# When VectorE adds a left tile to the running sum: a step after TensorE's use of it, or a step ahead of it

## What is computed

```python
x = x + ref(gn(x))
def ref(x, g_w, g_b, W_w, W_b, gamma, beta):
    g_x = einsum('oc,bchw->bohw', g_w, x) + g_b      # values, 128 channels
    f = einsum('bnc,bcm->bnm', theta, phi)           # theta = phi = x, 4096 x 4096
    attn = softmax(f, axis=-1)
    y = einsum('bnm,bmc->bnc', attn, g_x)
    wy = einsum('oc,bchw->bohw', W_w, y) + W_b
    wy = batchnorm(wy) * gamma + beta
    return wy + x
```

## Time and profile before

| | |
|---|---|
| time, median of 3 runs | 2401.73 us (2400.95 to 2404.8) |
| the profiled execution's own time | 2396.38 us |
| its span, first to last instruction | 2394.6 us |
| TensorE matmul busy | 2170.7 us, 91% |
| VectorE busy | 1690.0 us, 71% |
| ScalarE busy | 1085.4 us, 45% |
| GpSimd busy | 892.7 us, 37% |
| granted TensorE clock, mean | 0.975 |

### The profile page before, as it was taken

How to read it: one execution, slowest core, us unless ns; L and a number is a source line. 1 busy time by engine, 2 the same in 40 slices (tenths; PEclk the granted TensorE clock), 3 DMA queues, 4 the chain that set the end, 5 groups by cost and what they waited for, 6 DMA issues and landing times.

```text
span 2394.6 us, 32898 instructions
## 1 busy us (share of the span) xinstructions
PE 2170.7 (91%) x9520; PEld 1526.9 (64%) x9520; DVE 1690.0 (71%) x3062; ACT 1085.4 (45%) x2206; POOL 892.7 (37%) x624
## 2 busy tenths in 40 slices
PE   6899999997899999989889899998799999999878
PEld 4787766654587776655568677665458777665323
DVE  5565667878755666789766666787975576676876
ACT  3334445453444444445343444445434444444435
POOL 3001233568401013459531112346850102345860
PEclk9999999999999999999999999999999999999989
DMA  3121234544312223544412223353441232345869
GB/s 133 75 99 69 93 102 131 189 116 154 128 53 77 107 84 111 166 147 137 164 56 94 74 89 107 119 185 115 156 152 41 84 110 87 108 140 190 279 216 352
DMA packets 108412, 304.59 MB, mean 127 GB/s; under 512 B 11456, under 2 KB 11968, under 8 KB 93888
## 3 DMA queue, kind: packets, MB, share of 16 engines
q1 hardware_dynamic: 108224, 302.37, 37.4%
HBM read 159.71 MB, written 142.61 MB: 126 GB/s over the span
## 4 chain that ended last, share of the span: by engine, by line
PE 60%; POOL 15%; issue 13%; DVE 6%; ACT 3%; DMA 2%; DVEq 0%; SPq 0%; POOLq 0%; ACTq 0%
PE bank L1102 9%; PE bank L1104 8%; PE bank L1103 8%; PE bank L1157 8%; PE bank L1137 7%; POOL fy_d L674 5%; POOL fy_c L674 5%; PE bank L1161 4%; PE bank L1163 4%; PE bank L1162 4%; PE bank L1293 2%; ACT ring L740 2%; DVE lacc L956 2%; POOL xl L647 2%; PE bank L1223 2%
## 5 line engine op out<-in xcount | busy, mean ns | idle before, releaser
L766 ACT CAST phi<-bank 128x512 fp32r<-128x512 f32 x480 | 280.8, 587 | 905.1 <-PE bank L1137 904.9
L1102 PE MATMUL bank<-xh 128*128 128x512 f32 x1152 | 538.1, 467 | 38.8 <-DVE colmax L911 26.8
L903 DVE TENSOR_SCALAR_CACHE_REDUCE ring<-bank 128x512 f32<-128x512 f32 x576 | 395.1, 686 | 235.3 <-PE bank L1104 184.3
L1104 PE MATMUL bank<-xh,xl 128*128 128x512 f32 x1152 | 459.1, 399 | 0.0
L1103 PE MATMUL bank<-xl,xh 128*128 128x512 f32 x1152 | 456.1, 396 | 0.0
L1137 PEld LDWEIGHTS bank<-ident,ring 128*128 128x128 f32 x1920 | 237.5, 144 | 239.8 <-issue 141.0
L938 DVE TENSOR_TENSOR plo<-bank,phi 128x512 fp32r<-128x512 f32 x480 | 325.7, 683 | 90.8 <-ACT phi L766 56.2
L1137 PE MATMUL bank<-ident,ring 128*128 128x128 f32 x1920 | 301.7, 281 | 91.4 <-DVE plo L938 50.4
L674 POOL TENSOR_TENSOR fy_c<-fy_c,maxrow 128x512 f32<-128x512 f32 x200 | 294.1, 1472 | 188.5 <-DMA fy_c<-spill 188.3
L674 POOL TENSOR_TENSOR fy_d<-fy_d,maxrow 128x512 f32<-128x512 f32 x188 | 277.6, 1479 | 212.8 <-DMA fy_d<-spill 212.8
L740 ACT ACTIVATE ring<-ring,nmax 128x512 f32<-128x512 f32 x480 | 344.5, 719 | 0.0
(11 more groups left out here) (109 smaller groups left out, 2770.4 us busy)
## 6 DMA issues: line engine op xcount, KB each, us to landing
spill<-ring SPq DMA_DIRECT2D x112, 1024.0 KB, 4.4
fy_c<-spill SPq DMA_DIRECT2D x200, 256.0 KB, 4.0
fy_d<-spill SPq DMA_DIRECT2D x188, 256.0 KB, 3.7
ring<-x_dram SPq DMA_DIRECT2D x40, 512.0 KB, 4.8
lbuf<-spill SPq DMA_DIRECT2D x60, 256.0 KB, 4.1
yd<-yn SPq DMA_DIRECT2D x32, 256.0 KB, 3.2
fx_a<-x_dram SPq DMA_DIRECT2D x16, 512.0 KB, 7.2
out_dram<-fx_a SPq DMA_DIRECT2D x16, 512.0 KB, 4.5
```

Of the source, the lines that this page charges most:

```text
L903: last = nc.vector.tensor_scalar(ring[:, SLOT[u], t, :], src, 1.0, None, ALU.mult, ALU.max, accum_out=rowm[:, t, c:c + 1])
L1102: nc.tensor.matmul(dst, xh[:, k, rows], xh[:, k, cols], start=(k == 0), stop=False)
L1104: last = nc.tensor.matmul(dst, xl[:, k, rows], xh[:, k, cols], start=False, stop=(k == K - 1))
```

## The change

The addition of left tile w moves two steps earlier in VectorE's order: from the step after its use to the step before it (within its block). It no longer waits for TensorE's use, only for the exp. TensorE's use of a left tile now waits for the addition in place of the exp, except for a block's first two left tiles, which wait for the exp as before. The loads that reuse a buffer wait for the use (`tile_used`) in place of the addition; for a block's first two tiles, for the use of its third, since only that one waits for an addition.

```diff
-ADDS_AT = [[w for w in range(NLEFT) if min(LEFT[w] + 1, (LEFT[w] // TPB + 1) * TPB - 1) == p] for p in range(TILES)]
+def add_step(w):
+
+    return max(LEFT[w] - 1, LEFT[w] // TPB * TPB)
+
+
+ADDS_AT = [[w for w in range(NLEFT) if add_step(w) == p] for p in range(TILES)]
+
+
+def left_done(v):
+
+    return LEFT[max(v, LEFT_OF[LEFT[v] // TPB][2])] + 1
...
-                    sp.wait_ge(left_added, b * NLEFT + v + 1)
+                    sp.wait_ge(tile_used, b * TILES + left_done(v))
...
-                        if c < 2:
-                            sp.wait_ge(left_added, b * NLEFT + LEFT_NO[SLOT_USE[X_SLOT]] + 1)
-                        else:
-                            sp.wait_ge(tile_used, b * TILES + s)
+                        sp.wait_ge(tile_used, b * TILES + s)
                         load_x(b + 1, c)
...
                 dve.wait_ge(left_exp, b * NLEFT + w + 1)
-                dve.wait_ge(tile_used, b * TILES + LEFT[w] + 1)
...
-                    pe.wait_ge(left_exp, b * NLEFT + LEFT_NO[p] + 1)
+                    w = LEFT_NO[p]
+                    if w in LEFT_OF[j][:2]:
+                        pe.wait_ge(left_exp, b * NLEFT + w + 1)
+                    else:
+                        pe.wait_ge(left_added, b * NLEFT + w + 1)
```

More of the change, by code:

```diff
@@ L225 @@
 LAST_IN_SLOT = {k: max(u for u in range(len(CHUNKS)) if SLOT[u] == k) for k in range(SLOTS)}
+assert LEFT_NO[last_use(LAST_IN_SLOT[X_SLOT])] >= LEFT_OF[NB - 4][2]
 X_STEP = [last_use(LAST_IN_SLOT[X_SLOT + c // 2]) + 1 + c % 2 for c in range(NB)]
```

## The result

The changed kernel takes 2336.28 us (median of 4 runs, 2334.01 to 2344.38) against 2401.34 before (4 runs, 2396.69 to 2404.8): a ratio of 0.9743, 95% interval 0.9713 to 0.9773. The sign was right and the size was not: I had forecast 2381 and a range down to 2358. A later set of runs of the changed kernel gave 0.9743 again (0.9692 to 0.9795).

What follows compares the result with a forecast made beforehand. TensorE (busy 91%) was taken as the bound, GpSimd's subtractions in block 6 and the last image's blocks 6 and 7. 13 + 3.5 + 3.3 + 0.7 = 20.5 us off 2396.4 gave 2375.9; on the median's footing, 5.3 higher, 2381; range 2358 to 2403.

Steps and rivals of the forecast that it cites:

- So the sum is made of waits alone: Whole kernel: no compute instruction added or removed on TensorE, GpSimd, ScalarE or the DMA queue, so only waits change; 20.5 us.
- The terms for blocks 1 to 5: Five TensorE waits for VectorE in blocks 1, 4 and 5 of image 1 go or shrink: 6.6 us an image.
- I let two thirds through: Images 0 to 2: two thirds of the gain before the GpSimd-bound stretch survives, 3 x 6.6 x 2/3 = 13 us.
- Half for the last image: Last image: same places without the next image's statistics, so half the gain, 3.5 us.
- Block 6 of images 0 to 2: nothing: VectorE busy 63.9 and GpSimd 61.6 of 72.5 us, neither gets less to do: no gain, within 2 us of 72.5.
- The DMA queue: Last image, loads for block 7 behind a transfer awaiting block 6's additions: queue moves 3.3 us earlier, all 3.3 gained.
- The end: End of the last image: additions are done when the uses are, so the last uses end sooner, 0.7 us gained.
- the steady run: Last image's left runs: same GpSimd pace, each use later by about 1.5 us, once and not per tile.
- TensorE's new wait at zero: Uses of left tiles waiting for additions: cost taken as zero, at most 2.9 us on a tile here and there.
- nothing to see: Rival: VectorE's waiting was idle time of a non-binding engine; only the queue's 3.3 and end's 0.7 us stay: 2398, chance 0.14.
- the port rival: Block 5 from step 12 and block 6, images 0 to 2: TensorE pays for additions GpSimd slows; 2405 to 2430, chance 0.11.
- The third: Rival: all TensorE waits for VectorE shrink, three quarters of 80.4 us go, block 6 included: 2342, 2340 to 2362, chance 0.12.

Runs made afterwards that it cites:

- before with filling: Kernel before the change, with 3 to 8 small matmuls that change no sums put in front of seven of TensorE's regular waits: 2379.88 us, ratio 0.9895.
- the kernel with 204.5 us of VectorE's waiting: Kernel before the change, with each addition done on 32 of the 512 columns and the waits kept: 2281.85 us, ratio 0.9502.

## Why the prediction was wrong

The sum was 20.5 us and the span became 61.3 shorter. Images 0 to 2 gave 50.6 against my 13.

**"So the sum is made of waits alone."** This is the step that failed most. Behind many of the waits stood a second price: matmuls at the lower clock. Comparing blocks at a granted clock of 1.00 only (taken from before, or from before with filling), the waits alone are worth, per image: block 1, 1.9 us; block 4, 3.7; block 5, 0.5 (60.55 to about 60.1); block 6, 0.4 (71.27 to 70.87); block 7, 1.6; block 2, 0.1. That is 8.2 us, 24.6 in images 0 to 2, of the 50.6 us by which these images became shorter. Some of the six rest on a single block at that clock. The other 26 I put down to the clock, as what is left over. The filling shows that such a cause is there, apart from the waits: 23 us by the medians, 14 to 37 by the interval, with every wait still in place. The granted clock stood in the rows that I quoted (0.95 for block 6 in the earlier trace rows), and I did not ask what it cost.

**The terms for blocks 1 to 5.** Block 1's 1.94 us were right to the tenth. Block 4 was priced at 2.2 and gave 3.7: every gap of TensorE is closed. Block 5 was priced at 2.9 and gives 0.5 in images 0 to 2: the 1.34 us at step 6 are gone and the 2.62 at step 16 are 1.58 (I had left 1.0), but 4.4 us of new waits for additions stand in that block of image 1. The sum of 6.6 is 6.2 by measurement.

**"I let two thirds through."** Wrong: when blocks 1 to 5 alone are changed, blocks 6 and 7 take nothing back. Half for the last image was too little: 2.0, 2.7 and 3.9 us in blocks 1, 4 and 5 come to 8.6 against my 3.5, and some of that is clock (3.4 us of block 5 stood at the lower level before).

**"Block 6 of images 0 to 2: nothing."** Right for the wait alone (0.4), wrong for the block (2.4 in the mean of three). Block 7 of images 0 to 2 I did not cost at all; it gave 3.5.

**The DMA queue.** The place was right: from GpSimd's last subtraction of block 6 to the queue's move it was 6.49 us and is now 3.92, and GpSimd stands 2.96 us in place of 4.42. But block 7 did not become shorter, and its last use now trails the last subtraction by 5.0 us (2.4 before). Removed whole, the wait was worth 5.8 us there before the change; the 2.9 us after it can't be told from the block's own scatter.

**The end, and the steady run.** I had a gain of 0.7 us. The column sums now start 5.9 us after the last subtraction started, before 4.8, so it is a loss of 1.1. The use at 2314.34 in the earlier trace rows was the last and not the last but one, so no second use was left to come behind it as I had it. That uses would come later, once, was right, and 1.5 us was too little: the last one trails by 2.6 us more than before (5.0 and 2.4), by 1.7 more than where uses wait for the exp alone (3.3), and in the run ahead of it a use starts 7.3 us after its subtraction started (2246.14 and 2253.47) in place of 2.4. I had written it down as harmless and then added 0.7 for the very place where it falls due.

**TensorE's new wait at zero** held in the time (0.9746 without it), though not exactly: 0.8 us in each block 6 and about 1 us at the end, against the waits for ScalarE at the seams that it fills. That these nearly cancel is nothing that I had foreseen.

**The rivals.** The second, nothing to see, and the port rival did not come. The third came nearest (2342, its band 2340 to 2362), but not by its mechanism: three quarters of 80.4 us were to go, and 45.5 did, which is 57%. The rest was in good part the clock. I gave it too little because I looked at waits only where TensorE waits for VectorE by name; the 3.96 us for ScalarE at block 7's end, behind which the clock fell, is in no row of mine.

What stays open: why some short gaps bring a fall of the clock and equal ones don't. Before the change TensorE stood 1.83 us at step 30 of block 1 in each of images 0 to 2; the clock fell behind it in images 1 and 2 and not in image 0. The change leaves that gap as it is (1.83 us), and no fall follows it in the profile above. So falls became rarer also where the change left the gap, and "behind a wait that it removed" holds for block 7's seam but not for each fall. The mean clock of one kernel varies from run to run: 0.967 to 0.977 in seven runs of the kernel before. Open too: why the wait and the additions' length cost so much together, and what the filling costs where few falls are left.

## What to carry to other kernels

A wait of TensorE costs its own length and then, where the granted clock falls behind it, in places more than as much again (3.2 us for 2.0 in block 1): read the granted clock of each block's window, and the busy time of the same instructions in two windows, before summing waits. An engine that works ahead for another must not wait for it to catch up; put the wait on the engine that consumes, even if it then shows 84 us of waiting: here that cost nothing that could be measured. Sums of waiting are no price either way: the kernel with 204.5 us of VectorE's waiting was faster than the one with 134.4. Where a wait and the work behind it stand in one place, take each away alone and both together, and read the four by block: here the wait was nearly the whole cost in blocks 1 and 4, and the work in block 6.

## What the runs showed of the hardware

Matmuls that compute nothing, 33 in each image at seven places, made the kernel before the change 1.05% faster by keeping the granted clock up. A VectorE addition of 128x32 that took 0.17 us alone took 1.09 beside a GpSimd subtraction, to that one's end; with 512 columns the subtraction pays too (means of 1.29 us where no addition lies beside it and 1.55 where one does, in the kernel before; 1.29 and 1.28 with 32 columns). The additions' length is worth 70.7 us of the changed kernel's 2333.3, more than the change itself gained.
